# One product of the turned keys for both the inverted matrix and the query factor of a chunked delta rule

## The chip, the core and the metric

The kernel runs on one core of a Trainium2 chip. Its engines are TensorE (PE, with its weight loads as PEld), VectorE (DVE), ScalarE (ACT), GpSimd (POOL) and SyncE (SP), which here only issues DMAs. The metric is the device time of one execution in microseconds (us); lower is better.

## What is computed

The program chains a delta-rule attention layer, a mixture-of-experts layer, a selective scan and a gated feed-forward layer. The change touches the first alone. Its input is 4 sequences of 1024 tokens, 256 wide, two heads of 128. The reference works in chunks of 64 tokens, the kernel in chunks of 128. For each chunk and head:

```python
rk = rk / max(norm(rk), 1e-12);  wk = rk shifted by one token      # wk[t] = rk[t-1]
cum = cumsum(log_decay);  L_mask = tril(exp(tril(cum[:, None] - cum[None, :])))
M = tril(-(beta * wk @ wk.T) * L_mask, -1)
A = solve_triangular(eye - M, eye, lower=True, unit_diagonal=True)
intra = tril(rk @ wk.T * L_mask, -1)
v_new = A @ (v * beta) - A @ (wk * beta * exp(cum)) @ S
o     = (rk * exp(cum)) @ S + intra @ v_new
S     = exp(cum[-1]) * S + (wk * exp(cum[-1] - cum)).T @ v_new
out   = out + o @ W_read.T
```

The transposed query factor holds wk_i . rk_j. Since rk_j is wk_(j+1), the transposed M holds the same products one column further to the right.

## The kernel before, in words

**Passes.** `NSEQ` is 8: pass n treats chunk n of all four sequences (b = 0 to 3) and both heads (h). Most instructions of the stage come as one for each head, on a tile of 128 x 512 (4 sequences side by side). Each engine has its own program, written out by hand (`pe_a`, `dve_a`, `act_a`, `pool_a`, `sp_a`), and runs it in order; semaphores counted by step names (`g_pe`, `g_dve`, `g_act`, `g_pool`) tie them together. The order of the work is therefore the order of these texts. Each head has four PSUM banks, given out in turn along the list `order`: a step's bank is free when the step four places earlier has been read out (`gfree`).

**The matrix to be inverted.** For chunk n+1, made during pass n: PE forms `kk` = wk . wk^T (L994); DVE multiplies it with the decay factor E (`mix`, L545) and writes M. SP copies the eight 16 x 16 diagonal blocks out (`blocks`, eight DMAs md<-M, L317) and back, broadcast (`spread`, eight DMAs MB<-md, L325). POOL inverts these blocks (`solve`, 31 small steps on X and Y, L381 to L388). DVE spreads the result to DT (`inverse`, L551). In the next pass PE and DVE double the blocks from 16 to 128 in three levels (P4, D4, P5, D5, P6, T6), with transposed copies by ACT (`d4`, `t5`, `t6`); PE also turns M (`MT`) and ACT copies it (L916).

**The query factor.** PE forms `kq` = wk . rk^T at the end of pass n (`inner`); DVE multiplies it with ET (iT, L561). ET is the decay factor with its upper triangle selected by POOL (`upper`, L429).

**The decay factors.** ACT makes them out of the cumulated log decay of all keys, broadcast to all partitions by a DMA (`sums`, ZR<-cumd, L310; two DMAs of 256 KB). `lower(n+2)` makes E: eight Relu (L886) and two Exp (L891). `upper(n+1)` and `decays(n+1, "ET")` make ET: eight Relu (L900) and two Exp (L911). `decays(n+1, "ez")` makes ez = exp(cum) (L908), which POOL multiplies into rk (`decayed`, L439). SP issues `sums(n+2)` behind `spread(n+1)`, after ez(n+1) of both heads, since ZR has one buffer for each head.

**The end of a pass on ACT.** After `lower(n+2)` ACT copies the output o of pass n to OT (L974), computes the squares of keys (L798) and their roots (`roots`, L929). PE then forms the output product y (L1033) out of OT. At the top of pass n+1 DVE takes the reciprocal of the roots (`norms`, L571), adds y to XS (`residual_a`, L581) and only then does `mix`.

**Beside it.** POOL also scatters the tokens to the experts: from pass 2 on `scatter` issues indirect DMAs (L449), eight behind `solve` and four in the next pass after `mix` of head 1; the last sixteen stand together.

Of the kernel before, what the change touches and what calls it, by code (L numbers as in the profile page):

```python
# [39 lines left out]
def program(nc, x, wwT, wrT, alog0, dtb0, wh1, br1, wr2, br2, w1a, b1a, w2a, b2a,  # L40
            inT, convw, convb, xpT, dpT, dpb, alog1, dsk, opT,
            fch, f1s, f2s, g1s, g2s, f3s, out):
    with ExitStack() as ctx:
# [65 lines left out]
        sm = {k: sbt("sm_" + k, [P, NT, 2]) for k in ("beta", "nbeta", "g", "cum", "nbc", "ec", "bec", "tl", "tail", "ced")}  # L109
        sm.update({k: sbt("sm_" + k, [P, NT, 4]) for k in ("ab", "l")})  # L110
        S = sbt("S", [P, 2, B, P])
        nm = ["rk", "ez", "wk", "vsc", "E", "ET", "MT", "Dm", "DT", "Pm", "iT", "vn", "vnt"]
        TB = [{k: sbt(f"{k}{h}", [P, 4, P]) for k in nm} for h in range(2)]
        RD = [[sbt(f"rkdT{h}{i}", [P, 4, P]) for i in range(2)] for h in range(2)]
        M2 = sbt("M2", [P, 2, 4, P])
# [32 lines left out]
        cumT = sbt("cumT", [64, P])  # L148
        ZR = [sbt(f"ZR{h}", [P, 4, P]) for h in range(2)]
# [17 lines left out]
        a_dve = Count(sem("a_dve"), ["r2z", "r2i", "zt", "rnmax0", "rn0", "l0", "l1", "l2", "soft", "g0", "g1", "nbeta", "cum", "tl", "cumT", "ncum", "bec", "eye"])  # L167
# [16 lines left out]
        class Chunks:  # L184
# [9 lines left out]
            def at(self, name, n):  # L194
# [4 lines left out]
        order = ["kk'", "d4", "wkT", "wkS", "P4", "D4", "P5", "t5", "D5", "rkT''", "t6", "P6", "T6", "MT'", "vn", "v'", "o", "S", "kq'"]  # L199
        g_pe = [Chunks(sem(f"g_pe{h}"), ahead, order) for h in range(2)]  # L200
        g_dve = [Chunks(sem(f"g_dve{h}"), ["M", "vs", "iT", "DT"],
                        ["M'", *(("R", "P4") if h == 0 else ("P4", "R")), "D4", "P5", "D5", "P6", "T6", "vnt", "vs'", "S", "iT'", "DT'"]) for h in range(2)]
        g_act = [Chunks(sem(f"g_act{h}"), ["rk", "rT", "Er", "E", "ETr", "ez", "ET", "rk'", "MT", "rc", "rT'", "Er'", "E'"],
                        ["d4", "wk", "rk''", "ETr'", "ET'", "t5", "ez'", "rc'", "rT''", "t6", "MT'", "vn", "Er''", "E''", "o"]) for h in range(2)]
        g_pool = [Chunks(sem(f"g_pool{h}"), ["ETsel", "rkdT"], ["ETsel'", "rkdT'"]) for h in range(2)]
# [4 lines left out]
        cumd = nc.dram_tensor("cumd", [64, P], F32, kind="Internal").ap()  # L210
# [63 lines left out]
        def sp_a(e):  # L274
# [29 lines left out]
            def sums(n):  # L304

                for h in range(2):
                    if n > 1:
                        e.wait_ge(*g_act[h].at("ETr", n - 1))
                        e.wait_ge(*g_act[h].at("ez", n - 1))
                    e.dma_start(ZR[h][:], cumd.rearrange("(b n h) t -> n h b t", b=4, n=8)[n, h].rearrange("(o b) t -> o b t", o=1).to_broadcast([P, 4, P])).then_inc(s_zr, 16)  # L310

            def blocks(n):

                for h in range(2):
                    e.wait_ge(*g_dve[h].at("M", n))
# [18 lines left out]
            e.dma_start(cumd, cumT[:]).then_inc(s_zr, 16)  # L334
# [37 lines left out]
        def solve(e, n):  # L372

            for k in range(31):
# [9 lines left out]
                if k % 2:  # L384
                    e.tensor_tensor(Y16[:, :, r:15], MB[:, r:15, :, r].rearrange("p r g -> p g r"),
# [4 lines left out]
        def pool_a(e):  # L390
# [86 lines left out]
        def dve_a(e):  # L477
# [39 lines left out]
            e.wait_ge(*a_dve.at("soft"))  # L517
            e.wait_ge(*a_act.at("al"))
# [8 lines left out]
            e.tensor_copy(cumT[:], pb[6][0:64, 128:256]).then_inc(a_dve.sem, 1)  # L527
# [27 lines left out]
            def inner(n, h):  # L555
# [189 lines left out]
            for n in range(NSEQ):  # L745
# [35 lines left out]
                if more:  # L781
                    for h in range(2):
                        inner(n + 1, h)
# [6 lines left out]
        def act_a(e):  # L790
# [79 lines left out]
            def sums_of(n, h):  # L870
                return ZR[h] if n else gbank("z", 0, h)[:].rearrange("p (b m) -> p b m", b=4)
# [7 lines left out]
            def lower(n):  # L879
                for h in range(2):  # L880
# [4 lines left out]
                    for b in range(4):  # L885
                        t = e.activation(W["E"][:, b, :], z_[:, b, :], ACT.Relu, bias=sm["nbc"][:, n + 8 * b, h:h + 1])  # L886
# [16 lines left out]
            def decays(n, which):  # L903
                for h in range(2):
                    if which == "ez":
                        if n:
                            e.wait_ge(*g_pool[h].at("rkdT", n - 1))
                        e.activation(TB[h]["ez"][:], ZR[h][:] if n else four(gbank("z", 0, h)), ACT.Exp).then_inc(g_act[h].sem, 1)  # L908
# [26 lines left out]
            copy("MT", 0, "MT", "MT")  # L935
# [5 lines left out]
            lower(1)  # L941
            for n in range(NSEQ):
# [19 lines left out]
                if more:  # L962
                    copy("MT", n + 1, "MT", "MT")
# [16 lines left out]
        def pe_a(e):  # L980
# [1561 lines left out]
```

## Time and profile before

| | us |
|---|---|
| median of 3 runs | 2403.66 |
| lowest, highest | 2401.52, 2408.75 |
| the profiled execution | 2399.99 |
| its span | 2398.3 |
| PE, DVE, ACT, POOL busy in the span | 2197.5, 1843.5, 1646.8, 1449.4 |

The stage lies between about 55 and 405 us of the span; behind it come the experts and the scan, which the change does not touch. A busy share is a mean over all stages; what is to be read is which wait ends last within a pass. A timeline row is: start, length, engine, line, operation, out<-in, shapes, count, and in brackets the idle time before it with the releaser. Rows of equal instructions are merged.

### The profile page before, as it was taken

Reading aid. Unit: us, or ns where it says so; the run is one execution under the profiler, and the core shown is the slowest. Engines: PE = TensorE matmul, PEld = TensorE weight load, DVE = VectorE, ACT = ScalarE, POOL = GpSimd, SP = SyncE. Lnnn points to the kernel's source line nnn. Section 1 sums busy time; section 2 is a strip of 40 time slices with the busy share of each in tenths; the row PEclk is TensorE's granted clock in tenths of the full one; section 3 lists DMA queues with packets and bytes.
Section 4 is the critical chain, followed back from the end, with each engine's and each line's share of the span. In section 5 each row is a group of like instructions: output and inputs, shape, how many; then the busy total and the mean of one; then the engine's idle time right before and its main releaser. Section 6 shows DMA issues by size and latency. Waiting matters only on the chain.

```text
span 2398.3 us, 36952 instructions
## 1 busy us (share of the span) xinstructions
PE 2197.5 (92%) x12464; PEld 1788.7 (75%) x12464; DVE 1843.5 (77%) x2832; ACT 1646.8 (69%) x2715; POOL 1449.4 (60%) x1026
## 2 busy tenths in 40 slices
PE   6799897999999999996999999999999999999986
PEld 4788796998898898884667667676676765776765
DVE  5574453667766666677989989989899899898995
ACT  6775542555555556666887788787877877888774
POOL 0236563111111113336988989889889898898895
PEclk8899998999999999997999999999999999999988
DMA  8434544566666654444655655555555555565563
GB/s 291 85 56 111 112 125 136 181 236 232 234 230 230 233 209 152 133 126 154 219 169 190 198 184 186 194 186 202 176 186 195 199 187 177 185 211 177 178 208 101
DMA packets 235434, 430.22 MB, mean 179 GB/s; under 512 B 35089, under 2 KB 117457, under 8 KB 235234
## 3 DMA queue, kind: packets, MB, share of 16 engines
q1 hardware_dynamic: 229090, 410.87, 53.0%
q0 software_dynamic: 6144, 16.79, 2.2%
q8 instruction: 113, 1.85, 0.3%
q14 instruction: 87, 0.71, 0.1%
HBM read 353.61 MB, written 73.96 MB: 178 GB/s over the span
## 4 chain that ended last, share of the span: by engine, by line
PE 54%; DVE 13%; issue 9%; ACT 9%; DMA 6%; POOL 6%; SPq 1%; another core or an unknown queue 1%; POOLq 1%; DVEq 0%; ACTq 0%
PE pb L1641 11%; PE pb L1614 11%; DVE pb L2094 6%; PE pb L2406 5%; PE pb L2411 5%; PE pb L994 3%; PE pb L2305 2%; PE pb L2432 2%; PE pb L2321 2%; DVE UU L2100 2%; DMA XB<-xnd 2%; PE pb L2330 2%; DMA CC<-bcd 2%; POOL UU L2019 2%; POOL UU L2027 1%
## 5 line engine op out<-in xcount | busy, mean ns | idle before, releaser
L2019 POOL TENSOR_TENSOR UU<-dx,BB 128x1024 f32<-128x1024 f32 x256 | 614.6, 2409 | 112.0 <-DMA BB<-bcd 83.6
L2231 ACT ACTIVATE pb<-dt,al 128x512 f32<-128x512 f32 x512 | 339.5, 685 | 149.4 <-DVE UU L2100 147.8
L2100 DVE TENSOR_TENSOR UU<-pb,CC 128x512 f32<-128x512 f32 x512 | 351.3, 686 | 24.3 <-DMA CC<-bcd 6.5
L2094 DVE TENSOR_TENSOR_SCAN pb<-pb,hs,UU 128x512 f32<-128x512 f32 x256 | 328.5, 1283 | 10.7 <-ACT pb L2231 7.4
L2094 DVE TENSOR_TENSOR_SCAN pb<-pb,UU 128x512 f32<-128x512 f32 x256 | 313.0, 1223 | 8.5 <-ACT pb L2231 7.9
L1381 POOL TENSOR_TENSOR clo_b<-craw_b,chi_b 128x1024 fp32r<-128x1024 f32 x22 | 62.3, 2830 | 405.9 <-ACT chi_b L1444 405.9
L1531 DVE TENSOR_TENSOR HL<-HF,HH 128x512 fp32r<-128x512 f32 x220 | 159.6, 728 | 179.9 <-ACT HH L1436 165.7
L2406 PE MATMUL pb<-HAh,WH 128*128 128x512 f32 x1024 | 282.7, 419 | 7.0 <-DVE dt L2075 5.1
L1431 ACT ACTIVATE HF<-pb,BU 128x512 f32<-128x512 f32 x192 | 132.3, 689 | 219.4 <-PE pb L1614 191.9
L2411 PE MATMUL pb<-HAl,WH 128*128 128x512 f32 x1024 | 259.7, 396 | 0.0
L1641 PE MATMUL pb<-W2h,HH 128*128 128x256 f32 x880 | 256.0, 291 | 1.0
L1641 PE MATMUL pb<-W2l,HH 128*128 128x256 f32 x880 | 248.6, 282 | 0.0
L1641 PE MATMUL pb<-W2h,HL 128*128 128x256 f32 x880 | 248.5, 282 | 0.0
L2406 PEld LDWEIGHTS pb<-HAh,WH 128*128 128x128 f32 x1024 | 191.5, 193 | 67.2 <-issue 27.5
L2027 POOL TENSOR_TENSOR UU<-UU,UU 128x1024 f32<-128x1024 f32 x96 | 230.8, 2404 | 5.6 <-DVE UU L2100 5.6
L2411 PEld LDWEIGHTS pb<-HAl,WH 128*128 128x128 f32 x1024 | 195.4, 191 | 44.4
L2305 PEld LDWEIGHTS pb<-ident,UU 128*128 128x128 f32 x1280 | 147.7, 143 | 58.6 <-POOL UU L2027 38.5
L2305 PE MATMUL pb<-ident,UU 128*128 128x128 f32 x1280 | 165.5, 277 | 20.7 <-POOL UU L2027 19.9
L1641 PEld LDWEIGHTS pb<-W2h,HH 128*128 128x128 f32 x880 | 167.5, 190 | 12.0 <-DVE HL L1531 4.8
L1641 PEld LDWEIGHTS pb<-W2h,HL 128*128 128x128 f32 x880 | 167.8, 191 | 5.9 <-issue 1.0
L1641 PEld LDWEIGHTS pb<-W2l,HH 128*128 128x128 f32 x880 | 167.6, 190 | 0.0
L2045 POOL TENSOR_TENSOR HAl<-tg,HAh 128x512 fp32r<-128x512 f32 x128 | 162.9, 1297 | 5.4 <-ACT HAh L2269 5.4
(336 smaller groups left out, 4891.0 us busy)
## 6 DMA issues: line engine op xcount, KB each, us to landing
WH<-fhd SPq DMA_DIRECT2D x176, 512.0 KB, 3.5
BB<-bcd SPq DMA_DIRECT2D x256, 256.0 KB, 4.7
CC<-bcd SPq DMA_DIRECT2D x256, 256.0 KB, 5.0
raw<-in_w1a SPq DMA_DIRECT2D x23, 1024.0 KB, 7.3
raw<-in_w2a SPq DMA_DIRECT2D x23, 1024.0 KB, 7.4
craw_b<-in_fch SPq DMA_DIRECT2D x22, 512.0 KB, 5.9
fhd<-chi_b SPq DMA_DIRECT2D x22, 512.0 KB, 3.9
fld<-clo_b SPq DMA_DIRECT2D x22, 512.0 KB, 4.9
```

The lines of the kernel that those rows point to most:

```text
L1531: e.tensor_tensor(HH[q % 4][1][:], HF[q % 2][:], HH[q % 4][0][:].bitcast(F32), ALU.subtract).then_inc(s_hl, 1)
L1614: t = e.matmul(bk[:, a * wide:(a + 1) * wide], wt_[:, k, c_], xt_[k], start=(n == 0), stop=(n == 5))
L1641: t = e.matmul(to[:, j * D:(j + 1) * D], ht[:, c_], wt_[:, row, :], start=(row == 0 and j == 0 and m == 0), stop=(row == 7 and m == 2), sk ...
L2019: e.tensor_tensor(ubuf(n)[:], dx[p][:], BB[n % 3][:].rearrange("p (a m) -> p a m", a=1).to_broadcast([P, 2, 512]), ALU.mult).then_inc(p_u. ...
L2027: e.tensor_tensor(ubuf(n)[:], ubuf(n)[:], ubuf(n - 1)[:], ALU.add).then_inc(p_join.sem, 1)
L2045: e.tensor_tensor(hl[:, it, :], ttile("h", blk, j)[:], hh[:, it, :].bitcast(F32), ALU.subtract).then_inc(f_pool.sem, 1)
L2094: e.tensor_tensor_scan(h_[:], h_[:], uu[:, c, :], first, ALU.mult, ALU.add).then_inc(v_sc.sem, 1)
L2100: e.tensor_tensor(uu[:, c, :], abank(n, c)[:], CC[n % 3][:], ALU.mult).then_inc(v_mu.sem, 1)
L2231: e.activation(abank(n, c)[:], dt[p][:, c, :], ACT.Exp, scale=al1[:, 2 * p + c, s:s + 1]).then_inc(c_a.sem, 1)
L2305: t = e.matmul(ypart(j, c), ubuf(n)[:, c, j * P:(j + 1) * P], ident[:], is_transpose=True, start=False, stop=(s == 15), skip_group_check=True)
L2406: e.matmul(bk[:], WH[n % 3][:, c_], xh_, start=(k == 0), stop=False)
L2411: t = e.matmul(bk[:], WH[n % 3][:, c_], xl_, start=False, stop=(k == 7))
```

## The change

- For n of 1 and more `kk` and the turn `MT` are gone with its copy on ACT. `mix` reads the bank of `kq`, columns 0 to 126, times E columns 1 to 127, and writes the already transposed M (MTB, two buffers) straight. Chunk 0 keeps the old way.
- beta_i is now along the free axis: E(n) is relu of (cum_p - (cum - log beta)_j), from a second half of ZR. cumT, cumd and ZR hold two rows for one; PE makes the second with two more products, DVE its input `nl`. Each ZR DMA goes from 256 KB to 512 KB.
- `inner` moves on PE from the end of pass n to its top, in the place of `kk`; on DVE from the end of pass n to right behind `mix`. iT gets two buffers.
- `upper` and `decays(.., "ET")` on ACT move from the middle of pass n (for n+1) to the end of pass n (for n+2), between `lower(n+2)` and the copy to OT. On POOL `upper` moves behind `solve`.
- `solve` reads MB with the column innermost.

```diff
-        order = ["kk'", "d4", "wkT", "wkS", "P4", "D4", "P5", "t5", "D5", "rkT''", "t6", "P6", "T6", "MT'", "vn", "v'", "o", "S", "kq'"]
+        order = ["kq'", "d4", "wkT", "wkS", "P4", "D4", "P5", "t5", "D5", "rkT''", "t6", "P6", "T6", "vn", "v'", "o", "S"]
...
-                    upper(n + 1)
                     decayed(n + 1)
                     solve(e, n + 1)
+                    if n + 2 < NSEQ:
+                        upper(n + 2)
...
+                e.wait_ge(*g_pe[h].at("kq", n))
...
+                e.tensor_tensor(MTB[n % 2][:, h, :, 1:P], four(gbank("kq", n, h))[:, :, 0:P - 1], W["E"][:, :, 1:P], ALU.mult).then_inc(g_dve[h].sem, 1)
...
                     for h in range(2):
                         mix(n + 1, h)
+                    for h in range(2):
+                        inner(n + 1, h)
...
-                for h in range(2):
-                    inner(n + 1, h)
                     for h in range(2):
                         inverse(n + 1, h)
...
+                            t = e.activation(W["E"][:, b, :], ZR[h][:, b, 1, :], ACT.Relu, bias=sm["cum"][:, n + 8 * b, h:h + 1], scale=-1.0)
...
-                if more:
-                    upper(n + 1)
-                    decays(n + 1, "ET")
...
-                if more:
-                    copy("MT", n + 1, "MT", "MT")
                 copy("vn", n, "vn", "vn")
...
                 if n + 2 < NSEQ:
                     lower(n + 2)
+                    upper(n + 2)
+                    decays(n + 2, "ET")
                 for h in range(2):
                     e.wait_ge(*g_pe[h].at("o", n))
```

On ACT, from the copies of `t6` of pass 1 (DT) to the square roots. Before; vn is v_new:

```order
L916 ACTIVATE MT_97<-pb 128x512
L916 ACTIVATE MT_110<-pb 128x512
L916 ACTIVATE vn_102<-pb 128x512
L916 ACTIVATE vn_115<-pb 128x512
L886 ACTIVATE E_95<-ZR_164,sm_nbc 128x128 x4
L886 ACTIVATE E_108<-ZR_165,sm_nbc 128x128 x4
L891 ACTIVATE E_95<-E_95 128x512
L891 ACTIVATE E_108<-E_108 128x512
L974 ACTIVATE OT_125<-pb 128x512
L974 ACTIVATE OT_126<-pb 128x512
L798 ACTIVATE sq,rn<-XS 128x128 x8
```

The same place on ACT in the changed kernel:

```order
L928 ACTIVATE vn_101<-pb 128x512
L928 ACTIVATE vn_112<-pb 128x512
L896 ACTIVATE E_96<-ZR_164,sm_cum 128x128 x4
L896 ACTIVATE E_107<-ZR_165,sm_cum 128x128 x4
L903 ACTIVATE E_96<-E_96 128x512
L903 ACTIVATE E_107<-E_107 128x512
L912 ACTIVATE ET_97<-ZR_164,sm_cum 128x128 x4
L912 ACTIVATE ET_108<-ZR_165,sm_cum 128x128 x4
L923 ACTIVATE ET_97<-ET_97 128x512
L923 ACTIVATE ET_108<-ET_108 128x512
L987 ACTIVATE OT_125<-pb 128x512
L987 ACTIVATE OT_126<-pb 128x512
```

The two copies of MT are gone, and ten instructions on ET stand between E and OT.

On DVE, the seam between two passes, before (S is the state, DT<-X is `inverse`, XS<-pb is `residual_a`, M is `mix`):

```order
L778 SCALAR_TENSOR_TENSOR S<-S,sm_ced,pb 128x128 x8
L561 TENSOR_TENSOR iT_101<-pb,ET_96 128x512
L561 TENSOR_TENSOR iT_114<-pb,ET_109 128x512
L551 TENSOR_TENSOR DT_99<-X_123,mask 128x512
L551 TENSOR_TENSOR DT_112<-X_123,mask 128x512
L571 TENSOR_SCALAR rn<-rn 128x4x2
L573 RECIPROCAL rn<-rn 128x4x2
L581 TENSOR_TENSOR XS<-pb,XS 128x256 x4
L545 TENSOR_TENSOR M_121<-pb,E_95 128x512
L545 TENSOR_TENSOR M_121<-pb,E_108 128x512
```

The same seam on DVE in the changed kernel:

```order
L789 SCALAR_TENSOR_TENSOR S<-S,sm_ced,pb 128x128 x8
L560 TENSOR_TENSOR DT_99<-X_123,mask 128x512
L560 TENSOR_TENSOR DT_110<-X_123,mask 128x512
L580 TENSOR_SCALAR rn<-rn 128x4x2
L582 RECIPROCAL rn<-rn 128x4x2
L590 TENSOR_TENSOR XS<-pb,XS 128x256 x4
L554 TENSOR_TENSOR MTB_118<-pb,E_96 128x4x127
L554 TENSOR_TENSOR MTB_118<-pb,E_107 128x4x127
L570 TENSOR_TENSOR iTB_120<-pb,ET_97 128x512
L570 TENSOR_TENSOR iTB_120<-pb,ET_108 128x512
```

The two multiplications to iT moved from ahead of `inverse` to behind `mix`.

On ACT, from the copies of `t5` to ez in the changed kernel (pass 2 is alike):

```order
L928 ACTIVATE DT_110<-pb 128x512
L920 ACT_TABLE_LOAD
L920 ACTIVATE ez_93<-ZR_164 128x512
L920 ACTIVATE ez_104<-ZR_165 128x512
L877 ACTIVATE RKT<-RKT 128x4 x2
```

Before, ez follows the copy directly; the table load stands ahead of ET, before `t5`.

## Rows read from the trace of the kernel before

**Rows 1.** The page: busy time and share of each engine.

```profile
PE 2197.5 (92%) x12464; PEld 1788.7 (75%) x12464; DVE 1843.5 (77%) x2832; ACT 1646.8 (69%) x2715; POOL 1449.4 (60%) x1026
```

**Rows 2.** Busy by stretch: PE, PEld, DVE, ACT, POOL, clock, DMA share, GB/s.

```profile
127.00:162.00 35.00, 33.30 (x288) 31.83 (x287) 25.56 (x72) 23.05 (x64) 13.93 (x35) 1.00 0.36 61
```

**Rows 3.** The chain that ended last, pass 0: start, us, what.

```profile
103.03 11.26 DMA ZR<-cumd
...
114.62 2.14 ACT E L886 x7
...
117.80 0.97 ACT OT L974 x2
...
118.90 3.69 PE pb L1033 x16
```

**Rows 4.** ACT groups, 91 to 322 us: busy, mean ns, idle before, releaser.

```profile
L886 ACT ACTIVATE E<-ZR,sm_nbc 128x128 f32<-128x128 f32 x48 | 14.7, 388 | 28.7 <-DMA ZR<-cumd 28.7
...
L900 ACT ACTIVATE ET<-ZR,sm_cum 128x128 f32<-128x128 f32 x48 | 14.6, 394 | 0.0
...
L911 ACT ACTIVATE ET<-ET 128x512 f32<-128x512 f32 x12 | 6.9, 621 | 0.1
...
L974 ACT ACTIVATE OT<-pb 128x512 f32<-128x512 f32 x12 | 6.4, 577 | 1.0 <-PE pb L1166 1.0
...
L911 ACT ACT_TABLE_LOAD x5 | 6.4, 1283 | 0.1
```

**Rows 5.** Timeline of ACT, pass 1: the second copy of t5, and ez.

```profile
135.30 0.60 ACT L916 ACTIVATE DT<-pb 128x512 f32<-128x512 f32 x1 [0.67 <-PE pb L986]
135.79 1.14 ACT L908 ACTIVATE ez<-ZR 128x512 f32<-128x512 f32 x2
```

**Rows 6.** Timeline of SP's queue: pass 1, then pass 5.

```profile
126.61 5.05 SPq L317 DMA_DIRECT2D md<-M  x8
132.93 3.58 SPq L325 DMA_DIRECT2D MB<-md  x8
136.60 0.93 SPq L310 DMA_DIRECT2D ZR<-cumd  x2
...
304.83 0.94 SPq L310 DMA_DIRECT2D ZR<-cumd  x2
```

**Rows 7.** Timeline of DVE: M made for chunks 2, 6 and 7.

```profile
125.26 1.28 DVE L545 TENSOR_TENSOR M<-pb,E 128x512 f32<-128x512 f32 x2
...
284.25 1.28 DVE L545 TENSOR_TENSOR M<-pb,E 128x512 f32<-128x512 f32 x2
...
331.27 1.29 DVE L545 TENSOR_TENSOR M<-pb,E 128x512 f32<-128x512 f32 x2 [2.11 <-PE pb L986]
```

**Rows 8.** Timeline of PE, pass 4: turn of M; y; kk.

```profile
262.47 1.09 PE L986 MATMUL pb<-ident,M 128*128 128x128 f32 x8
...
277.89 3.69 PE L1033 MATMUL pb<-wr,OT 128*128 128x256 f32 x16 [1.82 <-ACT OT L974]
281.42 1.95 PE L994 MATMUL pb<-RKT 128*128 128x128 f32 x16
```

**Rows 9.** Timelines: last indirect DMA on POOL, and DVE around it.

```profile
381.32 0.96 POOL L449 DMA_INDIRECT xg<-rows,sl  x1 [0.31 <-issue]
...
384.78 1.29 DVE L726 TENSOR_TENSOR Pm<-pb,mask 128x512 f32<-128x512 f32 x2 [4.96 <-remote]
```

**Rows 10.** PE alone by stretch: busy, clock, DMA share, GB/s.

```profile
206.00:208.00 2.00, 0.00 (x0) 1.00 0.49 140
208.00:210.00 2.00, 0.00 (x0) 0.91 0.32 77
210.00:212.00 2.00, 1.75 (x8) 0.50 0.80 169
```

**Rows 11.** DMA issues: kind, count, KB each, median us to landing.

```profile
XS<-in_x SPq DMA_DIRECT2D x8, 512.0 KB, 6.4
...
ZR<-cumd SPq DMA_DIRECT2D x14, 256.0 KB, 9.9
```

**Rows 12.** Timeline of DVE, pass 3: the first level after M.

```profile
209.50 1.29 DVE L726 TENSOR_TENSOR Pm<-pb,mask 128x512 f32<-128x512 f32 x2 [3.51 <-remote]
```

More of the change, by code:

```diff
@@ L109, in program @@
         sm = {k: sbt("sm_" + k, [P, NT, 2]) for k in ("beta", "nbeta", "g", "cum", "nbc", "ec", "bec", "tl", "tail", "ced")}
+        sm["nl"] = sbt("sm_nl", [P, NT, 2])
         sm.update({k: sbt("sm_" + k, [P, NT, 4]) for k in ("ab", "l")})
         S = sbt("S", [P, 2, B, P])
-        nm = ["rk", "ez", "wk", "vsc", "E", "ET", "MT", "Dm", "DT", "Pm", "iT", "vn", "vnt"]
+        nm = ["rk", "ez", "wk", "vsc", "E", "ET", "Dm", "DT", "Pm", "vn", "vnt"]
         TB = [{k: sbt(f"{k}{h}", [P, 4, P]) for k in nm} for h in range(2)]
         RD = [[sbt(f"rkdT{h}{i}", [P, 4, P]) for i in range(2)] for h in range(2)]
-        M2 = sbt("M2", [P, 2, 4, P])
+        MTB = [sbt(f"MTB{i}", [P, 2, 4, P]) for i in range(2)]
+        iTB = [sbt(f"iTB{i}", [P, 2, 4, P]) for i in range(2)]
         MB = sbt("MB", [P, 15, 8, 16])
@@ L147, in program @@
         rows = [sbt(f"rows{i}", [P, 2, D]) for i in range(3)]
-        cumT = sbt("cumT", [64, P])
-        ZR = [sbt(f"ZR{h}", [P, 4, P]) for h in range(2)]
+        cumT = sbt("cumT", [64, 2, P])
+        ZR = [sbt(f"ZR{h}", [P, 4, 2, P]) for h in range(2)]
         a_end = at[0]
@@ L333, in sp_a @@
             e.wait_ge(*a_dve.at("cumT"))
-            e.dma_start(cumd, cumT[:]).then_inc(s_zr, 16)
+            e.dma_start(cumd, cumT[:].rearrange("p k t -> p (k t)")).then_inc(s_zr, 16)
             e.wait_ge(s_zr, 16)
@@ L907, in decays @@
                             e.wait_ge(*g_pool[h].at("rkdT", n - 1))
-                        e.activation(TB[h]["ez"][:], ZR[h][:] if n else four(gbank("z", 0, h)), ACT.Exp).then_inc(g_act[h].sem, 1)
+                        e.activation(TB[h]["ez"][:], ZR[h][:, :, 0, :] if n else four(gbank("z", 0, h)), ACT.Exp).then_inc(g_act[h].sem, 1)
                     else:
@@ L934, in act_a @@
             rows_(1)
-            copy("MT", 0, "MT", "MT")
+            for h in range(2):
+                e.wait_ge(*g_pe[h].at("MT", 0))
+                e.activation(MTB[0][:, h], four(gbank("MT", 0, h)), ACT.Copy).then_inc(g_act[h].sem, 1)
             carried(0)
@@ L941, in act_a @@
             lower(1)
+            upper(1)
+            decays(1, "ET")
             for n in range(NSEQ):
@@ L1104, in pe_a @@
                 if more:
-                    for h in range(2):
-                        e.wait_ge(*g_act[h].at("rc", n))
-                        kk(n + 1, h)
+                    inner(n + 1)
                 for h in range(2):
@@ L1147, in pe_a @@
                         e.matmul(bk[:, 256:512], ones[:], mv_, start=True, stop=True).then_inc(s_cnt8, 1)
-                if more:
-                    for h in range(2):
-                        MT(n + 1, h)
                 for h in range(2):
@@ L1171, in pe_a @@
                         product("S", n, h, W["wk"], W["vnt"])
-                if more:
-                    inner(n + 1)
                 for b2 in range(2):
```

65 lines of the change are left out of this document (38 added, 27 removed).

## The prediction, made before the changed kernel ran

> **What bounds the kernel now.** The page comes first: PE is busy for 92% of the span [rows 1], and a stretch of one pass shows the same, 33.30 of 35.00 us at full clock [rows 2]. That suggests that PE work removed is time removed. The chain of waits says otherwise, so it is read second. In pass 0 it runs through the DMA of the sums, 11.26 us, then ACT's E, then OT, then PE's product y [rows 3]. Over six passes ACT idles 28.7 us before E, all of it for that DMA, and 1.0 us for PE before OT [rows 4]: OT comes when ZR's landing allows, nearly never when PE does. In pass 4 PE itself waits 1.82 us for OT ahead of y [rows 8].
>
> The loop, followed in pass 1: M at 125.26 [rows 7], blocks out at 126.61, back in at 132.93, ZR issued at 136.60 [rows 6]: 11.3 us after M. ZR lands about 12.4 us later (in pass 0 11.26 us pass from the second of the two issues). E takes 3.4 us, OT 1.05. From OT's end (118.75 in pass 0, 277.74 in pass 4, by what follows it in [rows 3] and [rows 8]) to the next M (125.26, 284.25) [rows 7] is 6.5 us in both: eight squares, a table load and the roots on ACT, then norms and residual on DVE, with y and kk beside them on PE. 11.3 + 12.4 + 3.4 + 1.05 + 6.5 is about 34.7 us, and undisturbed passes last 35.5 to 38. So two things are nearly equal, PE's work and this loop, and the loop is the longer. Whoever shortens PE gains nothing; whoever lengthens the loop pays in full.
>
> **Removed.** For each of seven chunks PE loses kk (1.78 us without the overlap of the last one, printed 1.95) and the turn of M (0.88, printed 1.09) [rows 8]: 2.7 us a pass, 18.6 us in all. On the loop neither counts: kk's place is taken by kq, which M now waits for at the same spot, and the turn stands ahead of vn, whose branch ends before OT. I cost it at nothing; the cover is ACT's wait for ZR. Without that cover it would be -18.6 us. The two MT copies on ACT (1.1 us a pass) lie in the same idle time and count nothing. In mid-pass ET is gone ahead of t5; but in pass 1 the second t5 waits 0.67 us for PE [rows 5], so ACT arrives early enough already: nothing.
>
> **Moved, ET.** Now ten instructions stand between E and OT. They read ZR, so they can't start before it lands, and E waits for the same landing. Over six passes (0 to 5) they cost 14.6 + 6.9 = 21.5 us [rows 4], 3.6 us a pass, all on the loop. Off that goes the 1.0 us that OT waited for PE. **Term: +20.5 us.** OT then is some 4 to 8 us later than PE's o, so PE idles ahead of y in each pass.
>
> **Moved, the table.** The Exp table was loaded (1.28 us) ahead of ET, before t5 [rows 4]. Now the first Exp after the roots is ez, behind t5, on a stretch where ACT was only just in time. ZR for n+2 is issued after ez(n+1). In pass 1, ZR went out at 136.60, when ez of head 0 was just done (135.79 plus 0.6) [rows 5, 6]; SP's own queue was free at 136.5. One microsecond later for ez is one for ZR. Passes 2 to 5 pay (in pass 1 another Exp, of the routing, takes the load while ACT waits): four by 1.28, less 0.6 where SP had been the later one. **Term: +4.5 us.**
>
> **Moved, the start.** ET of chunk 1 now stands ahead of the copy d4 of pass 0. That delays P4 by about 3.6 us and, with the 1.1 us that ACT had in hand there and no table load, ez(1) and ZR(2) by about 1.7. **Term: +1.7 us.**
>
> **Moved, DVE.** `inner` (1.3 us) stands ahead of the carry of head 0. PE's P4 waits for it too, by the turn of the banks. M starts 6.5 us after OT, iT is complete at 9.1; PE needs y, kq, d4, wkT and wkS first, 3.5 + 1.8 + 0.9 + 0.9 + 1.8 = 8.9. Nothing, at most 0.3 a pass. POOL's select now follows solve; ET is ready before the next M by 7.5 us, so `inner` does not wait for it.
>
> **Doubled, ZR.** No row shows a 512 KB ZR. From below: it has the same number of packets, each twice as long, and XS<-in_x, 512 KB each, lands in 6.4 us where ZR's 256 KB take 9.9 [rows 11]; by that it costs nothing. From above: if its time went with its bytes, the 11.3 us of the pair could double, +60 us in six passes; but the 512 KB row contradicts that. I take 0 and keep up to 2 us a pass for the range. The Trainium skill (DMA: Bandwidth & Descriptors, Why small descriptors are slow) says that each packet carries a fixed overhead, which would make doubled packets cost less than twice; by its overhead alone the sum stays as it is. That is in line with the 512 KB row; no run here shows it yet. The second row of cumT with two small products and `nl` in front is at most 0.5 us.
>
> **Beside it, the scatter.** Late in a run of indirect DMAs every hand-over between engines gets slow: in pass 3 DVE waits 3.51 us for a product long done [rows 12], in the last pass 4.96 us, up to just after the last indirect DMA at 381.32 [rows 9]. Such disturbance is why passes 3 and 5 take 47 us, like 284.25 to 331.27 [rows 7]. The select of ET now holds POOL until after OT is nearly due, so the eight start some 4 us later against solve, and the next four follow without a gap. I read the old disturbances that lay ahead of M (some 3 us twice) as gone, and one behind M (8 us) as added: about 0 to +2, with -20 and +12 as ends. After the last M, solve (30 us) and sixteen indirect DMAs (20 us) follow as before, so the end shifts with it. **Term: 0.**
>
> **Sum.** 20.5 + 4.5 + 1.7 + 0 = 26.7 us on the profiled execution's 2399.99: 2426.7. The median of the runs is 3.7 above that execution, so for the median I give 2430.
>
> **Rivals.** (1) *PE is the bound*, as the busy share says, and ET fits into ACT's idle time. The page's 92% [rows 1] speaks for it, the 28.7 us of idle ahead of E [rows 4] at first sight too; against it is that this idle time ends with the landing of what ET itself reads. It would give 2403.66 - 18.6 = 2385, faster. (2) *The disturbance goes.* If the later indirect DMAs meet an idle PE and slow nothing, the 8 + 3 + 8 + 3 us of passes 3 to 6 are saved: 2430 - 22 = 2408, no change or nearly. For it: PE will idle where the run begins. Against: the run lasts 15 us, longer than that idle time. (3) *The clock falls.* After an idle stretch of 4.3 us at 206 to 210 us PE's granted clock went from 1.00 to 0.50, 2.4 to 1.2 GHz [rows 10]; after 1.82 us at 277.89 it did not, y took its 3.69 [rows 8]. With 4 to 8 us of idle ahead of y, y and what follows up to t5 would take up to 3.4 us more a pass, on the loop through t5, ez and ZR: +20 us in six passes, less where the disturbance covers it, so 2450. The Trainium skill (TensorE: Matmul & The Clock Gate, Part 1) says that the clock of an engine left idle is halved. By that rule, the trace agrees at 206 to 212 us, and the time would come nearer 2450 than 2430. (4) *ZR's bytes count*, 2 us a pass: 2442, or 2460 with (3).
>
> The rival that ends on the other side is (1); it decides if OT still follows PE's o within 2 us.
>
> **How the numbers follow.** The forecast as it stands, 2415 to 2442: 0.58. (3) and (4), 2442 to 2465: 0.22. (2), 2400 to 2415: 0.13. (1): 0.07. The range that holds 8 in 10 goes from 2408 to 2458. About 0.3%, 7 us, can be told from no change. Below 2396.5 lies (1), 0.07; within 7 us about 0.09 of (2); above it 0.84.
>
> **What would show it.** Right: on ACT, E, ET and OT in one piece right after ZR lands, and OT before y as PE's releaser in every pass, with 4 to 8 us idle; ZR issued 12.5 us or more after M instead of 11.3; passes of 39 to 50 us; PE's busy time about 18 us less; ZR landing as before, 10 us. Wrong: y released by PE's own order; the stage ending before 405 us; or the extra time lying behind 405 us. Should the granted clock read 0.5 right after y in most passes, (3) adds to it. If PE's idle time is there but the end comes no later, the scatter has given it back.

## The result, and the profile after

| | before | after |
|---|---|---|
| median of 5 runs, us | 2403.66 | 2433.80 |
| lowest, highest | 2400.01, 2414.59 | 2425.38, 2434.81 |
| span of the profiled execution | 2398.3 | 2432.0 |
| M of chunk 2 / of chunk 7, start in the trace | 125.26 / 331.27 | 132.93 / 358.91 |

The ratio is 1.0111, with a 95% interval from 1.0087 to 1.0134: the kernel became slower by 30 us, 2430 having been forecast.

The page of after, busy time of the engines:

```profile
PE 2187.8 (90%) x12300; PEld 1777.6 (73%) x12300; DVE 1838.8 (76%) x2833; ACT 1638.9 (67%) x2701; POOL 1442.0 (59%) x1026
```

It would be hard to see the loss there: against [rows 1] PE has 164 instructions and 9.7 us less. One pass shows what happened. The timeline of ACT in pass 4 of after (start, length, engine, line, operation, operands, count, and in brackets the idle time before it with its releaser):

```profile
298.01 2.45 ACT L896 ACTIVATE E<-ZR,sm_cum 128x128 f32<-128x128 f32 x8 [7.21 <-DMA ZR<-cumd]
300.37 1.13 ACT L903 ACTIVATE E<-E 128x512 f32<-128x512 f32 x2
301.40 2.43 ACT L912 ACTIVATE ET<-ZR,sm_cum 128x128 f32<-128x128 f32 x8
303.74 1.13 ACT L923 ACTIVATE ET<-ET 128x512 f32<-128x512 f32 x2
304.78 1.05 ACT L987 ACTIVATE OT<-pb 128x512 f32<-128x512 f32 x2
```

And the timeline of PE in after, y of passes 0 to 4:

```profile
125.75 6.20 PE L1046 MATMUL pb<-wr,OT 128*128 128x256 f32 x16 [4.60 <-ACT OT L987]
...
166.16 3.69 PE L1046 MATMUL pb<-wr,OT 128*128 128x256 f32 x16 [2.90 <-ACT OT L987]
...
211.46 6.01 PE L1046 MATMUL pb<-wr,OT 128*128 128x256 f32 x16 [6.59 <-ACT OT L987]
...
256.97 5.45 PE L1046 MATMUL pb<-wr,OT 128*128 128x256 f32 x16 [6.35 <-ACT OT L987]
...
305.98 6.53 PE L1046 MATMUL pb<-wr,OT 128*128 128x256 f32 x16 [6.87 <-ACT OT L987]
```

E, ET and OT run in one piece behind the landing of ZR, and y starts 0.15 us after OT ends, in all six passes from 0 to 5. In before only pass 4 had a wait of note there [rows 8]. These are the rows on ACT, 91 to 353 us, that answer to [rows 4] (busy, mean ns, idle before, releaser):

```profile
L896 ACT ACTIVATE E<-ZR,sm_cum 128x128 f32<-128x128 f32 x48 | 14.7, 388 | 35.3 <-DMA ZR<-cumd 35.3
...
L987 ACT ACTIVATE OT<-pb 128x512 f32<-128x512 f32 x12 | 6.3, 575 | 0.0
L920 ACT ACT_TABLE_LOAD x4 | 5.1, 1283 | 0.1
```

In these passes OT never waits for PE any more. M of chunk 2 and of chunk 7 (head 0) on DVE, which answer to [rows 7]:

```profile
132.93 0.69 DVE L554 TENSOR_TENSOR MTB<-pb,E 128x508 f32<-128x508 f32 x1 [0.19 <-issue]
...
358.91 0.69 DVE L554 TENSOR_TENSOR MTB<-pb,E 128x508 f32<-128x508 f32 x1 [0.19 <-issue]
```

ZR's issue in pass 1 on SP's queue [rows 6], and the DMA issues with KB and median us to landing [rows 11]:

```profile
145.74 0.93 SPq L312 DMA_DIRECT2D ZR<-cumd  x2
```

```profile
ZR<-cumd SPq DMA_DIRECT2D x14, 512.0 KB, 10.7
XS<-in_x SPq DMA_DIRECT2D x8, 512.0 KB, 5.9
```

**Where the 34 us of the trace came from.** The loop can be cut at four points, and summed over its six rounds from M of chunk 1 to M of chunk 7:

| stretch, six rounds, us | before | after | difference |
|---|---|---|---|
| M to the issue of ZR | 91.1 | 100.8 | +9.7 |
| issue of ZR to E | 77.3 | 76.6 | -0.7 |
| E to the end of OT | 27.8 | 46.9 | +19.1 |
| end of OT to the next M | 45.3 | 44.0 | -1.3 |
| sum | 241.5 | 268.4 | +26.8 |

With 0.8 us ahead of the first M the last M is 27.6 us late. Another 6.5 us lie behind it: from there to the first turn of the experts' rows are 76.5 us in before (331.27 to 407.72) and 83.0 in after (358.91 to 441.90). From that point on the two kernels run alike; the spans differ by 33.7 us.

### The profile page after: what moved, and what is told of

It reads as the page before. It is cut to its first block, busy times and chain, and to the rows that moved or that the text cites. A ratio compares the mean times of both kernels' runs of the same rounds, so it can differ in the third digit from the quotient of the medians.

```text
span 2432.0 us, 36582 instructions
## 1 busy us (share of the span) xinstructions
PE 2187.8 (90%) x12300; PEld 1777.6 (73%) x12300; DVE 1838.8 (76%) x2833; ACT 1638.9 (67%) x2701; POOL 1442.0 (59%) x1026
## 4 chain that ended last, share of the span: by engine, by line
PE 50%; DVE 12%; issue 10%; ACT 10%; DMA 8%; POOL 7%; SPq 1%; POOLq 1%; another core or an unknown queue 0%; DVEq 0%; ACTq 0%
PE pb L1652 12%; PE pb L1625 11%; DVE pb L2105 6%; PE pb L2417 4%; PE pb L2422 4%; DMA ZR<-cumd 3%; POOL UU L2030 2%; PE pb L2332 2%; PE pb L2443 2%; DVE UU L2111 2%; PE pb L1007 2%; PE pb L2341 2%; PE pb L2316 2%; DMA XB<-xnd 2%; POOL UU L2038 2%
## 5 line engine op out<-in xcount | busy, mean ns | idle before, releaser
L2105 DVE TENSOR_TENSOR_SCAN pb<-pb,hs,UU 128x512 f32<-128x512 f32 x256 | 328.4, 1283 | 13.1 <-ACT pb L2242 9.0
L2422 PEld LDWEIGHTS pb<-HAl,WH 128*128 128x128 f32 x1024 | 193.6, 189 | 43.5
L2316 PE MATMUL pb<-ident,UU 128*128 128x128 f32 x1280 | 165.7, 278 | 23.0 <-POOL UU L2038 22.1
## 6 DMA issues: line engine op xcount, KB each, us to landing
BB<-bcd SPq DMA_DIRECT2D x256, 256.0 KB, 4.7
CC<-bcd SPq DMA_DIRECT2D x256, 256.0 KB, 4.9
```

The source lines that it names most:

```text
L2105: e.tensor_tensor_scan(h_[:], h_[:], uu[:, c, :], first, ALU.mult, ALU.add).then_inc(v_sc.sem, 1)
L2316: t = e.matmul(ypart(j, c), ubuf(n)[:, c, j * P:(j + 1) * P], ident[:], is_transpose=True, start=False, stop=(s == 15), skip_group_check=True)
L2422: t = e.matmul(bk[:], WH[n % 3][:, c_], xl_, start=False, stop=(k == 7))
```

## The experiments

They ran in three sets. Each set had one chip, and the kernel before ran on it too: 2358.55 us in the first set, 2401.16 in the second, 2402.28 in the third. So only ratios are compared between sets.

### First set: which part costs it

**b_et_end**: before, with ET moved as in the change, and nothing else of it. There is still a kk, a turn of M and a ZR of 256 KB. What goes with ET's place goes with it: the Exp table is loaded ahead of ez, and POOL's select stands behind `solve`.

```diff
-                if more:
-                    upper(n + 1)
-                    decays(n + 1, "ET")
...
                 if n + 2 < NSEQ:
                     lower(n + 2)
+                    upper(n + 2)
+                    decays(n + 2, "ET")
                 for h in range(2):
                     e.wait_ge(*g_pe[h].at("o", n))
```

> The kernel before with one part of the change alone: ET for chunk n+2 at the end of pass n, between E and OT, with two buffers for ET and the select behind solve; kk, the turn of M and the old places of kq and iT are kept. Loop theory: the whole loss comes from this part and the PE work saved is worth nothing, so 24 to 32 us over the kernel before, as slow as the changed kernel. Rival 'PE counts as well': by the 18.6 us of kk and turn slower than the changed kernel, 45 us over before. Rival 'ET's place does not matter': as before.

Measured: 2391.46 us, ratio 1.0130 (1.0092 to 1.0168), the loss of the whole change. ACT in its pass 4:

```profile
280.72 2.45 ACT L889 ACTIVATE E<-ZR,sm_nbc 128x128 f32<-128x128 f32 x8 [5.76 <-DMA ZR<-cumd]
283.08 1.14 ACT L894 ACTIVATE E<-E 128x512 f32<-128x512 f32 x2
284.12 2.43 ACT L903 ACTIVATE ET<-ZR,sm_cum 128x128 f32<-128x128 f32 x8
286.45 1.14 ACT L914 ACTIVATE ET<-ET 128x512 f32<-128x512 f32 x2
287.49 1.05 ACT L978 ACTIVATE OT<-pb 128x512 f32<-128x512 f32 x2
```

It is the same piece as in after. The position of ET alone gives the loss. That the PE work which the change removes gives nothing back while ET stands there, the times show only roughly, since the interval reaches 9 us to either side. The traces of this set are closer: the experts start at 396.3 us in b_et_end and at 395.6 in a_table below, which is the whole change with the table loaded elsewhere.

**b_zr512**: before, with ZR written at 512 KB.

```diff
-        ZR = [sbt(f"ZR{h}", [P, 4, P]) for h in range(2)]
+        ZR2 = [sbt(f"ZR{h}", [P, 4, 2, P]) for h in range(2)]
+        ZR = [z_[:, :, 0, :] for z_ in ZR2]
```

> The kernel before with ZR doubled alone: each DMA of the sums 512 KB instead of 256 KB (the second half is a copy that nothing reads). If a DMA costs by its packets: ZR lands after 9.9 to 10.5 us in the median as before and the time is within 3 us of before. If bytes count: landing 2 to 11 us later, 12 to 60 us slower.

Measured: 2355.78 us, ratio 0.9992 (0.9978 to 1.0007). Its DMA issues:

```profile
ZR<-cumd SPq DMA_DIRECT2D x14, 512.0 KB, 9.5
```

Twice the bytes in the same number of packets cost nothing; b_et_end's 256 KB took 9.8 us beside it. Rival (4) is out.

**a_otfirst**: after, with the copies OT ahead of ET, and the norms behind `inner`.

```diff
-                if n + 2 < NSEQ:
-                    norms(n + 2)
...
                         inner(n + 1, h)
+                if n + 2 < NSEQ:
+                    norms(n + 2)
...
-                    upper(n + 2)
-                    decays(n + 2, "ET")
...
                     e.activation(OT[h][:], four(gbank("o", n, h)), ACT.Copy).then_inc(g_act[h].sem, 1)
+                if n + 2 < NSEQ:
+                    upper(n + 2)
+                    decays(n + 2, "ET")
```

> The changed kernel, with ACT's copy of o to OT ahead of ET instead of behind it, and DVE's reciprocal of the roots behind the query factor. Loop theory (ET between E and OT lengthens a closed loop by 3.6 us a pass): PE waits for OT under 2 us instead of 2.9 to 6.9, and M follows OT by 4.5 to 6.5 us; 20 to 30 us faster than the changed kernel, so about 2403 to 2412. Rival 'PE's and DVE's new order (P4 waits for iT, the query factor ahead of the carry) is the cause': within 5 us of the changed kernel, about 2430.

Measured: 2369.10 us, ratio 1.0047 (1.0033 to 1.0062). That is 0.0072 to 0.0083 below a_table and b_et_end of the same set, 17 to 20 us, just short of what was expected; that PE would wait under 2 us for OT was a miss. PE's wait for OT in the list of waits of a_otfirst, then of b_et_end:

```profile
PE pb L1047 <- ACT OT L985: 15.8, 6, 3.9
```

```profile
PE pb L1037 <- ACT OT L978: 17.7, 7, 3.8
```

The sums are nearly alike, and yet the six rounds of the loop take 229.9 us in a_otfirst and 244.1 in b_et_end, and the stretch from E to the end of OT in them 27.0 against 46.9. PE, without kk and the turn, comes to y earlier and waits again. Some 60% of the loss go with the two moves together. Which part of it is the norms', no run shows: M follows OT by 4.8 us in passes 0 to 2, where after took 6.5 to 8.5. OT is behind E alone now, and through E still behind ZR: PE waits 3.1 to 3.9 us in each of passes 2 to 5.

**a_table**: after, with a small Exp ahead of t5 in passes 2 to 5, so that the table is loaded there and not ahead of ez.

```diff
                 if n + 2 < NSEQ:
                     rows_(n + 2)
+                    if n >= 2:
+                        e.activation(dum[:], al[:, 0:1], ACT.Exp)
```

> The changed kernel with one small Exp ahead of t5 in passes 2 to 5, so that the table load runs while ACT waits for PE instead of ahead of ez. Loop theory: ZR goes out 1.28 us earlier in four passes, about 5 us faster than the changed kernel. Rival 'ez is not on the path': no change.

Measured: 2387.06 us, ratio 1.0119 (1.0079 to 1.0158). From M to ZR's issue it takes 12.9, 13.1 and 12.4 us in passes 3, 4 and 5. No run of this set has the changed kernel with the load ahead of ez and M in the same place: a_otfirst takes 13.8 us there, but 13.8 in pass 1 as well, where no load stands ahead of ez. So neither the trace nor the time shows the microsecond: inconclusive for a term of 4 us.

### Second set: take ZR off the loop

**a_again** is the changed kernel once more, as the second set's own reference.

> The changed kernel once more, as the reference for the three beside it: 24 to 32 us over the kernel before; PE waits 3 to 7 us for OT in passes 0 to 5.

Measured: 2433.38 us, ratio 1.0131 (1.0104 to 1.0158).

**b_zr2**: before, with two buffers for ZR, so that ZR for chunk n+2 is issued at the top of pass n and not after ez(n+1).

```diff
+                if n + 2 < NSEQ:
+                    sums(n + 2)
                 if n + 1 < NSEQ:
                     blocks(n + 1)
                 if n + 1 < NSEQ:
                     spread(n + 1)
-                if n + 2 < NSEQ:
-                    sums(n + 2)
```

> The kernel before with the landing of ZR taken off the loop: two buffers for each head, and the sums for chunk n+2 issued at the top of pass n, ahead of the blocks. Loop theory: ACT no longer waits for ZR, OT follows PE's o, and only what PE waited for OT comes back, 0 to 2 us a pass: 2 to 8 us faster than before. Rival 'the loop was no bound': no change.

Measured: 2398.92 us, ratio 0.9986 (0.9974 to 0.9998). The list of waits of b_zr2:

```profile
ACT OT L976 <- PE pb L1168: 27.7, 14, 4.8
```

Of these 27.7 us 20.9 lie in passes 0 to 5, where in [rows 4] ACT waited 28.7 us for ZR and 1.0 for PE. With ZR early it still waits, now for PE's o. So ZR's loop was the longer one, and PE's work came right behind it: 3 us of gain.

**a_zrearly**: the same on after, but with one buffer, which is free early because ez(n+2) moves to the end of pass n, behind OT.

```diff
+                    if n + 2 < NSEQ:
+                        decays(n + 2, "ez")
...
                 if n + 2 < NSEQ:
                     sums(n + 2)
                 if n + 1 < NSEQ:
                     blocks(n + 1)
```

> The changed kernel with the landing of ZR taken off the loop: ez for chunk n+2 at the end of pass n behind OT, the sums for chunk n+2 issued at the top of pass n. Loop theory: E and ET run before PE's o is there, ET costs nothing, the 2.7 us a pass of kk and turn show: 10 to 18 us faster than the kernel before, about 40 us faster than the changed kernel, 8 to 16 faster than the one before with two ZR buffers. Rival 'PE's new order with P4 behind iT holds it': within 3 us of before.

Measured: 2417.50 us, ratio 1.0063 (1.0039 to 1.0087). A miss: 16 us better than after, but not faster than before. The first reading was that ZR, issued just ahead of md and MB, delays the solve, since the largest row of the waits now is this one:

```profile
POOL X L384 <- DMA MB<-md: 100.5, 7, 21.5
```

That reading was wrong. POOL waits long only because rkdT, its work ahead of the solve, is now done early. What counts is how long after MB's issue the solve starts: 9.4 us in passes 0, 1 and 2 of a_zrearly (pass 2: 179.27 and 188.68), 9.4 in before (98.88 and 108.27). Only in pass 0 does ZR stand in the way: SP holds md back until ez is done, MB goes out at 107.76 and not at 98.88, and pass 1 lasts 43.5 us. Where the rest went, the third set shows.

**a_best**: a_zrearly with OT ahead of ET and the squares, roots and norms of the keys one chunk earlier.

> As the one with the early ZR, and besides OT ahead of ET and the squares, roots and norms of the keys made one chunk earlier, so that M waits for neither. Loop theory: M then follows OT by 4.5 us instead of 6.5, but PE's own work is the bound: within 4 us of it, rather faster.

Measured: 2420.48 us, ratio 1.0073 (1.0049 to 1.0096), no better than a_zrearly, and within the 4 us of it that were expected.

### Third set: a second pair of ZR buffers, and the clock

**a_zr2**: after, with a second ZR for each head. One lies in TM0, which is not loaded before the last pass, one in the router's hidden rows. ZR for chunk n+2 is issued at the top of pass n, as in b_zr2; ez stays where it was.

```diff
+        ZRB = [[TM[0][:].rearrange("p a (k t) -> p a k t", k=2), ZR[0][:]], [HB[:], ZR[1][:]]]
...
-                    e.dma_start(ZR[h][:].rearrange("p b k t -> p b (k t)"), cumd...
+                    e.dma_start(ZRB[h][n % 2].rearrange("p b k t -> p b (k t)"), cumd...
```

> After, with a second pair of buffers for ZR (the memory of TM0, not yet loaded, and that of the router's hidden rows), so that ZR for chunk n+2 is issued at the top of pass n, ahead of md and MB, and long before ScalarE comes to E. ez keeps its place in the middle of the pass. Theory (the loss is that E, ET and OT run in one piece behind ZR's landing, and y waits for OT): ScalarE's E waits for ZR under 3 us in all (after: 30.4 in five passes), TensorE's wait for OT falls from 33 us in six passes to under 8, y is back at 3.7 us, and the saved product and turn (3.1 us in a pass) can show: 5 to 16 us faster than before, ratio 0.993 to 0.998. Rival (what the products of the turned keys wait for, the inverse behind P4 on VectorE, eats it): within 3 us of before, ratio 0.999 to 1.001. Rival (ZR ahead of md and MB delays the solve, as where ez came late): GpSimd waits over 50 us for MB and the ratio stays over 1.004.

Measured: 2410.54 us, ratio 1.0035 (1.0021 to 1.0050). As a forecast of the time it is a miss: 5 to 16 us faster than before was expected. The timeline of ACT at the end of pass 1:

```profile
152.00 2.43 ACT L919 ACTIVATE ET<-ZR,sm_cum 128x128 f32<-128x128 f32 x8
154.34 1.14 ACT L930 ACTIVATE ET<-ET 128x512 f32<-128x512 f32 x2
155.38 0.58 ACT L994 ACTIVATE OT<-pb 128x512 f32<-128x512 f32 x1
156.17 0.60 ACT L994 ACTIVATE OT<-pb 128x512 f32<-128x512 f32 x1 [0.22 <-PE pb L1186]
```

The mechanism is gone: E has no wait for ZR from pass 0 on, y has none for OT, and it takes 3.69 us in every pass. Some 70% of the loss went with it, about 20 us. The rest, 8 us over before, has another place. Here y starts 36.16 us after y in pass 1 (before: 37.55), but 44.9, 44.5, 44.5 and 43.0 us in passes 3 to 6 (before: 43.5, 40.4, 45.3 and 36.7). The timeline of DVE in pass 4:

```profile
249.24 1.27 DVE L577 TENSOR_TENSOR iTB<-pb,ET 128x512 f32<-128x512 f32 x2
260.45 1.13 DVE L733 SCALAR_TENSOR_TENSOR vsc<-pb,sm_bec,vsc 128x128 f32<-128x128 f32 x4 [9.94 <-remote]
```

The last indirect DMA of that pass on POOL:

```profile
257.46 0.96 POOL L459 DMA_INDIRECT xg<-rows,sl  x1 [0.31 <-issue]
```

And PE, the product that waits for DVE:

```profile
262.23 3.78 PE L1014 MATMUL pb<-Pm,DT 128*128 128x128 f32 x16 [9.74 <-DVE Pm L742]
```

DVE waits 9.94 us for a product that PE had long made, until 2 us after the last of twelve indirect DMAs, and PE then runs the next level at half clock (3.78 us; 2.05 in pass 1). It is the disturbance that the prediction took from [rows 12], nearly three times its size. Another part of the rest is smaller: in pass 1 PE waits for DVE ahead of the first level, where before had no gap.

```profile
132.71 2.05 PE L1014 MATMUL pb<-Pm,DT 128*128 128x128 f32 x16 [1.17 <-DVE Pm L742]
```

**a_zr2b**: a_zr2 with OT ahead of ET, and squares, roots and norms one chunk earlier. **b_best**: b_zr2 with the latter.

> The same with the copies OT ahead of ET's Relu and Exp on ScalarE, and the squares, roots and norms of the keys one chunk earlier. Theory: with ZR there early, ET ahead of OT cost at most a few us in a pass, and OT is ready before TensorE wants it: 1 to 8 us faster than the same kernel without these two. Rival: nothing there waits any more, within 2 us of it; or the moved norms push VectorE's inverse back, up to 5 us slower.

> Before, with two ZR buffers issued at the top of the pass, and squares, roots and norms one chunk earlier: the same loop without the shared product. Two ZR buffers alone gave 0.9986 beside its own before; the earlier norms may add 0 to 4 us. Theory (in a loop that does not wait for ZR the shared product is worth its TensorE time): 5 to 14 us slower than the version with the shared product of this call. Rival (the shared product is worth nothing): within 3 us of it.

The squares and norms one chunk earlier change nothing in b_best. Measured: a_zr2b 2425.00 us, ratio 1.0082 (1.0056 to 1.0107); b_best 2402.06 us, 0.9999 (0.9980 to 1.0017). Both are misses. With OT first, ET ends later, and so do POOL's select and the indirect DMAs behind it: they start 4.2 us behind y in pass 2, and 1.5 us in a_zr2. DVE's waits grow to 8.9 and 13.9 us in passes 3 and 4. The version without the shared product is again the faster one, by 8 us against a_zr2. No version was found that beats before by more than b_zr2's 3 us.

**a_warm**: after, with nine products of 128x128 ahead of each bank of y, to keep PE busy while it waits for OT.

```diff
                 e.wait_ge(*gfree("y", n, b2))
+                for _ in range(9 if n + 2 < NSEQ else 0):
+                    e.matmul(bk[:, 0:P], ones[:], ident[:], start=True, stop=True)
```

> After, with nine products of 128x128 (results overwritten) ahead of each y bank in passes 0 to 5, while TensorE would wait for OT. The clock's part of the loss: y took 5.5 to 6.5 us in five of six passes of after where it took 3.7 before. If the idle time ahead of y lets the clock fall, y is back at 3.7 to 4.5 us, M follows OT's end by 6.5 us, and the kernel is 5 to 12 us faster than after (ratio 1.006 to 1.010). If the fall has another cause, y stays at 5.5 or more and the ratio at 1.011 or more; fillers that outlast the wait would cost up to 2 us in a pass.

Measured: 2427.76 us, ratio 1.0111 (1.0094 to 1.0128), not to be told from after. PE in its pass 2:

```profile
202.90 2.17 PE L1043 MATMUL pb<-ident,ones 128*128 128x128 f32 x18
209.68 3.75 PE L1048 MATMUL pb<-wr,OT 128*128 128x256 f32 x8 [4.61 <-ACT OT L987]
213.22 2.99 PE L1043 MATMUL pb<-ident,ones 128*128 128x128 f32 x18
216.05 1.89 PE L1048 MATMUL pb<-wr,OT 128*128 128x256 f32 x8
```

The products were too few and ended 4.6 us before OT came: the first bank of y still ran at half clock (3.75 us for eight), the second at full (1.89), and the second lot of products cost as much as it saved. This run decides nothing on the price of the clock; that is read from the trace of after, below.

## Why the prediction was right

**The bound.** That ZR's loop and not PE sets the pass was the step on which all rests, and b_et_end and b_zr2 show it from both sides. Rival (1) is out: it wanted OT behind PE's o, and y starts 0.15 us behind OT in every pass.

**ET, +20.5 us.** Measured +19.1 from E to the end of OT. Confirmed, by a_otfirst and b_et_end too. The passes, M to M, last 39.6 to 50.9 us (39 to 50 forecast), and ZR goes out 12.8 us or more after M, as forecast; y waits 2.9 to 6.9 us, where 4 to 8 had been forecast.

**The table and the start, +4.5 and +1.7.** The stretch from M to ZR's issue grew by 9.7 us, of which 1.9 lie in pass 0. That is near the 1.7 forecast, though how these come out of 3.6 and 1.1 us the prediction does not show. In passes 2 to 5 the load is there (four of 1283 ns, 5.1 us). In pass 1 nothing was forecast, and 1.5 us came (12.8 against 11.3): they belong to the clock, see below. Pass 2 took 3.6 us more, of which 1.3 are the load; the rest belongs to DVE and to the clock behind its wait, also below. Passes 3 to 5 together took 2.8 us more, and how these divide is open: disturbances of 5 to 9 us fall into this stretch in both kernels, in different passes.

The timeline of ACT in pass 2 of after shows the load ahead of ez:

```profile
187.83 0.60 ACT L928 ACTIVATE DT<-pb 128x512 f32<-128x512 f32 x1 [0.73 <-PE pb L999]
188.44 1.28 ACT L920 ACT_TABLE_LOAD   x1
189.74 1.15 ACT L920 ACTIVATE ez<-ZR 128x512 f32<-128x512 f32 x2
```

From the end of the copy to ez it costs 1.3 us. The Trainium skill (ScalarE: Activation LUTs, What ACT_TABLE_LOAD costs) gives about 1283 ns for the load, which the trace repeats, and about 1380 ns more for a drain, 2.66 us for a switch. The trace does not agree with the second part, and the row decides.

**Removed, 0.** Right for this change: b_et_end, which removes nothing, loses the same within its interval. PE's busy time fell by 9.7 us and not by 18, since y alone took 33.4 us in six passes at a partly halved clock, where 3.69 each would be 22.1. The two add up to 21.0.

**Moved on DVE, at most 0.3 us a pass.** Here the size was off. The sum ended at PE's P4; the level after it waits for Pm, and ahead of Pm on DVE stand now `inner` and, in pass 2 of both kernels, 4.8 us of routing work. PE in pass 2 of before:

```profile
169.03 2.05 PE L994 MATMUL pb<-Pm,DT 128*128 128x128 f32 x16 [1.86 <-DVE Pm L726]
```

PE in passes 1 and 2 of after:

```profile
138.94 2.05 PE L1007 MATMUL pb<-Pm,DT 128*128 128x128 f32 x16
...
181.45 3.28 PE L1007 MATMUL pb<-Pm,DT 128*128 128x128 f32 x16 [4.50 <-DVE Pm L735]
```

In pass 2 it waits 4.50 us in the place of 1.86, and then takes 3.28 us in the place of 2.05, with the granted clock at 0.50, 1.2 GHz, from 182 us on. Counted from M, the level starts 1.0 us later than in before. In pass 1 of after there is no wait, because the slow y before it makes PE the later one; in a_zr2, where y takes 3.69, PE waits 1.17 us at this place, and its pass 2 lasts 39.9 us against 37.5.

**ZR doubled, 0.** Confirmed by b_zr512 to within 0.2%. (The upper end that was ruled out, 11.3 us six times, is 68 us and not 60.) The issue-to-E stretch did not grow.

**Scatter, 0, with -20 and +12 as ends.** Inside the loop DVE's idle times of over 3 us that belong to it fell from 12.5 us (3.5, 9.0) to 5.8; behind the last M, in pass 6, before has none and after this one:

```profile
369.67 1.13 DVE L726 SCALAR_TENSOR_TENSOR vsc<-pb,sm_bec,vsc 128x128 f32<-128x128 f32 x4 [5.65 <-remote]
```

It ends 1.8 us after a run of twelve indirect DMAs without a gap. From the last M to y of that pass it takes 28.6 us in before and 35.8 in after; the last pass, with its sixteen in one row [rows 9], is as long in both (40.8 and 40.1 us from y to y). So pass 6 holds the 6.5 us behind the last M that the sum did not have. "After the last M ... as before" was the step that failed, and it is most of what separates 26.7 from the 34 us of this trace. Rival (2) is answered by the first set: its chip shows hardly any of the disturbance, and the ratios of b_et_end and a_table there (1.0130 and 1.0119) are like those of the whole change on the other chips (1.0111 and 1.0131).

**The clock, rival (3).** It happened, at about a third to a half of its price. PE alone in after, around y of pass 3 (busy, granted clock, DMA share, GB/s):

```profile
256.00:257.00 1.00, 0.03 (x1) 0.50 0.00 0
257.00:259.00 2.00, 2.00 (x5) 0.50 0.19 66
259.00:261.00 2.00, 2.00 (x8) 0.62 0.23 80
261.00:264.00 3.00, 3.00 (x23) 1.00 0.35 122
```

After 6.35 us of idle time PE runs at 0.50, 1.2 GHz, and is back at 1.00, 2.4 GHz, before y ends. Five of six y's took 5.45 to 6.53 us. But M follows OT by 6.51 us because of ACT's and DVE's work, beside which y had room: OT to M took 7.3, 6.5, 8.5, 6.6, 8.5 and 6.6 us, 4.9 us more than six times 6.51. That is not all of it, since PE's work behind y is late as well. In pass 1 neither a table load nor a disturbance hides this. From the start of y at 125.75, which took 6.20 us, PE works without a gap and comes to the first level at 138.94, 13.2 us later; before needed 10.8 (118.90 to 129.69), with y at 3.69. ZR goes out 20.1 us after OT in place of 17.9: 0.8 us of the 2.3 lie ahead of M and 1.5 behind it. b_et_end supports it: there pass 0's y took 3.69 us, and pass 1 needs 11.4 us from M to ZR's issue, like before. So the slow y's cost some 6.4 us at least, and at most the 11.3 by which they were longer. The prediction had charged up to 3.4 us a pass, 20 in all, on the view that the low clock would last up to t5.

Ahead of M, before had 6.3 us of disturbance in two passes (9.97 and 9.31 us in the place of 6.51) that after has not, so the stretch as a whole is 1.3 us shorter.

In sum: 26.7 forecast, less 1.4 for ET, plus 3.5 for the stretch from M to ZR's issue, less 1.3 and 0.7 in the two other stretches, plus 0.8 ahead of the first M and 6.5 behind the last one, gives the 34.1 us by which the experts start later in the trace. The medians are 30.1 apart. The sum held because its largest term did; what it lacked behind the loop is as large as its two smaller terms together. That the median came within 4 us of 2430 is in part luck: the disturbance alone had been given ends 32 us apart, and the trace has it at neither.

## What to carry to other kernels

Where an engine idles ahead of a step, look at what ends that idle time before you put work into it: ACT idled 28.7 us ahead of E, but the work that was moved there read the same DMA, so it added its full length. A busy share of 92% does not make PE the bound, and two loops of nearly equal length (here ZR's, and PE's own work 3 us behind it) hide each other: taking work off one shows nothing until the other is shortened too. And the largest wait in a list is not a cause until the step behind it is late: 100 us of POOL waiting for MB in a_zrearly meant only that POOL had nothing else to do.

## What the runs showed of the hardware

**Twelve indirect DMAs in a row hold up hand-overs, in two of the three sets.** POOL issues them every 1.27 us. In the second and third set, and in the traces of before and after above, a run of twelve with no gap over 2 us held DVE for 3.5 to 14 us, mostly over 7, and the last such wait ended 1.3 to 2.9 us after the last of them. Where the last four came 2.2 us or more behind the first eight, no wait was longer than 4.0 us. Before had two runs of each kind in passes 2 to 5, a_zr2 four of the first. Idle times of this kind sum to 40 us there and to 12.5 in before, 28 more, while a_zr2 lost only 8. These sums are no measure of what the disturbance costs, though. b_zr512, as fast as before on its own chip, comes to the first turn of the experts' rows at 366.5 us in the first set, and before at 407.7 in the trace above: 41 of the 47 us between the two spans lie in this stage. What the shared product is worth with ZR off the loop and without the disturbance is open: a_zr2 did not run on the first set's chip.

In the first set the same runs of twelve held DVE nowhere (while they ran, it waited over 3 us only for the roots and for y, which both come behind OT). The timeline of a_otfirst, DVE in pass 4, while POOL issued indirect DMAs from 241.0 to 256.0:

```profile
244.83 1.28 DVE L570 TENSOR_TENSOR iTB<-pb,ET 128x512 f32<-128x512 f32 x2
...
246.46 1.13 DVE L726 SCALAR_TENSOR_TENSOR vsc<-pb,sm_bec,vsc 128x128 f32<-128x128 f32 x4
248.25 0.69 DVE L735 TENSOR_TENSOR Pm<-pb,mask 128x512 f32<-128x512 f32 x1 [0.66 <-PE pb L1008]
```

It is the same stretch of the program as in a_zr2's rows above: 0 us of wait here, 9.94 there. What differs between the chips stays open, and so does what holds the engines. PE is held as well. The timeline of PE in pass 3 of a_zrearly, where POOL issued from 204.8 to 220.0:

```profile
217.72 0.40 PE L1010 MATMUL pb<-Dm,MTB 128*128 128x128 f32 x2 [1.29 <-issue]
218.43 0.27 PE L1010 MATMUL pb<-Dm,MTB 128*128 128x128 f32 x1 [0.32 <-issue]
219.84 0.37 PE L1010 MATMUL pb<-Dm,MTB 128*128 128x128 f32 x1 [1.14 <-issue]
```

The products of one level come singly, with gaps in which PE waits for nothing that the profile shows. The Trainium skill (SBUF — State Buffer, SBUF: two separate sides) says that DVE and POOL share a pair of ports under an exclusive lock, and that PE has its own. By that rule only DVE or POOL could be held; the gaps on PE do not agree with it, so it can't be the whole of it.

That a run with a gap is harmless was seen, not tried: no kernel here put a gap into a run that had none. It is the first thing to try next, on a_zr2, beside a_zr2 as it is on a chip like the first set's.
